# The copies of the transposed ternary weights move from VectorE to ScalarE

## The chip, the cores and the metric

The kernel runs on the 8 cores of one Trainium2 chip, the same program on each, each with 2 of the 16 sequences. All cores prepare the same weights for themselves. The metric is the device time of the slowest core in microseconds (us).

## The reference

A layer: layernorm, then a Nystrom attention and a feed-forward block with quantized weights and activations, both added to x.

```python
x  = L0_attn_x                                   # (16, 2048, 1024)
xn = _layernorm(x)
x  = x + attn(xn, Wk, Wq, Wv, Wo, bo) + ffn(xn, w1, conv_w, conv_b, w2)

def weight_quant(w):                             # w1 is (4096, 1024), w2 is (1024, 4096)
    scale = 1.0 / clip(mean(abs(w)), 1e-05)
    return clip(round(w * scale), -1, 1) / scale

def ffn(x, w1, conv_w, conv_b, w2):
    h = einsum('bsd,hd->bsh', act_quant(x), weight_quant(w1))
    h = silu(depthwise_conv1d(h, conv_w, conv_b))
    return einsum('bsh,dh->bsd', act_quant(h), weight_quant(w2))
...
```

The change touches `weight_quant` alone: the ternary weights (-1, 0, 1) are made once, before both sequences, and are needed with their input dimension on the partitions, so they are transposed.

## The kernel before

A core first prepares weights, then runs five stages for each of its two sequences, with a barrier of all engines and all DMAs after the preparation and after each stage. The generator `prep_weights` casts the four attention matrices (32 pieces) while `phase_A` (layernorm and quantization of sequence 0) is emitted in between; by the time it comes to w1 and w2, phase A is over. Then `_tern_weight` runs for w1 and for w2, alone on the core.

`_tern_weight` works on chunks of 128 rows: 32 chunks of 128x1024 for w1, 8 chunks of 128x4096 for w2. It has two passes over the weights, each of which loads every chunk from HBM by a DMA on SP's queue into one of two buffers `wtmps[c % 2]`; the load of chunk c+1 is emitted before the work on chunk c, and waits until the buffer's last reader is done.

Pass 1: VectorE sums the absolute values of each chunk (L398). Then two small matmuls and some one-element operations (L404 to L440) give the scale. Pass 2, for each chunk c, emitted in this order:

1. ScalarE: `w * scale + C_RND` in place, so that the value is rounded (L453).
2. VectorE: subtract `C_RND`, write int16 `ti` (L457).
3. VectorE: clip to -1..1, write bf16 `tb` (L460).
4. TensorE: for each group of 8 blocks of 128x128, 8 transposes into one PSUM bank (L470). w1 has one group for a chunk, always in `pb[2]`; w2 has four, in `pb[2]` and `pb[3]` in turn.
5. VectorE: copy the group's 128x1024 bf16 from PSUM to SBUF, for w1 into the resident `w1t` (L479, a strided destination), for w2 into the buffer `stage` (L485).
6. w2 only: one DMA of `stage` to `w2t_sp` in HBM, issued from ScalarE's queue (L490, listed as L162 in the trace, the line of the DMA helper).

There is no planner: what an engine runs, and in which order, is the order in which these calls are emitted. The helper `op` puts, ahead of an instruction, a wait for each writer and reader of its buffers, those on the same engine included: the four copies of a w2 chunk all write `stage`, so each waits for the end of the one before. After w2 comes the barrier, and then `phase_B1` of sequence 0, whose first instruction is a memset (L697).

Of the kernel before, what the change touches and what calls it, by code (L numbers as in the profile page):

```python
# [46 lines left out]
class Builder:  # L47
# [331 lines left out]
    def _tern_weight(self, wd, nrows, ncol, is_w1, tern_bufs):  # L379
        nc = self.nc  # L380
        nch = nrows // 128
        wtmps, ti, tb, stage = (tern_bufs[k] for k in
                                ("wtmp", "ti", "tb", "stage"))
        absacc = Buf(self.sml.ap[:, 448:448 + nch], "absacc")
        if is_w1:
            self._absacc = absacc
        else:
            absacc = self._absacc
        def ldw(c):
            self.dma(Buf(wtmps[c % 2].ap[:, 0:ncol], "wtv"),  # L390
                     wd[c * 128:(c + 1) * 128, :], writes=(wtmps[c % 2],))

        ldw(0)
        for c in range(nch):
            if c + 1 < nch:
                ldw(c + 1)
            wtmp = wtmps[c % 2]
            self.op("dve", lambda c=c, wtmp=wtmp: nc.vector.reduce_sum(  # L398
                absacc.ap[:, c:c + 1], wtmp.ap[:, 0:ncol], axis=AX.X,
                apply_absolute_value=True),  # L400
                reads=[wtmp], writes=[absacc])
            yield
        ps = self.pb[0]
        self.op("pe", lambda: nc.tensor.matmul(  # L404
            ps.ap[:1, 0:nch], self.ones_col.ap, absacc.ap[:, 0:nch],
            start=True, stop=True),
            reads=[self.ones_col, absacc], writes=[ps])
        tot = Buf(self.sml.ap[:1, 1700:1701], "tot")
        self.op("dve", lambda: nc.vector.reduce_sum(
            tot.ap, ps.ap[:1, 0:nch], axis=AX.X), reads=[ps], writes=[tot])  # L410
        mean = Buf(self.sml.ap[:1, 1701:1702], "mean")
        self.op("dve", lambda: nc.vector.tensor_scalar(
            mean.ap, tot.ap, 1.0 / (nrows * ncol), 1e-5, ALU.mult, ALU.max),
            reads=[tot], writes=[mean])
        scale = Buf(self.sml.ap[:1, 1702:1703], "scale")
        self.op("dve", lambda: nc.vector.reciprocal(scale.ap, mean.ap),
                reads=[mean], writes=[scale])
        row2 = Buf(self.sml.ap[:1, 1704:1706], "row2")
        self.op("dve", lambda: nc.vector.tensor_copy(row2.ap[:, 0:1], scale.ap),
                reads=[scale], writes=[row2])  # L420
        self.op("dve", lambda: nc.vector.tensor_copy(row2.ap[:, 1:2], mean.ap),
                reads=[mean, row2], writes=[row2])
        ones_row = Buf(self.sml.ap[:1, 1708:1836], "ones_row")
        self.op("dve", lambda: nc.vector.memset(ones_row.ap, 1.0),
                writes=[ones_row])
        ps2 = self.pb[1]
        self.op("pe", lambda: nc.tensor.matmul(
            ps2.ap[:, 0:2], ones_row.ap, row2.ap, start=True, stop=True),
            reads=[ones_row, row2], writes=[ps2])
        if is_w1:  # L430
            self.w1_mw = Buf(self.sml2.ap[:, 229:230], "w1_mw")
            self.w1_sc = Buf(self.sml2.ap[:, 230:231], "w1_sc")
            mw_col, sc_col = self.w1_mw, self.w1_sc
        else:
            self.w2_mw = Buf(self.sml2.ap[:, 231:232], "w2_mw")
            self.w2_sc = Buf(self.sml2.ap[:, 232:233], "w2_sc")
            mw_col, sc_col = self.w2_mw, self.w2_sc
        self.op("dve", lambda: nc.vector.tensor_copy(sc_col.ap, ps2.ap[:, 0:1]),
                reads=[ps2], writes=[sc_col])
        self.op("dve", lambda: nc.vector.tensor_copy(mw_col.ap, ps2.ap[:, 1:2]),  # L440
                reads=[ps2], writes=[mw_col])
        if is_w1:
            self.cw2 = Buf(self.sml2.ap[:, 128:128 + 3 * NHC], "cw2")
            self.op("dve", lambda: nc.vector.tensor_scalar(
                self.cw2.ap, self.cw.ap, mw_col.ap, None, ALU.mult),
                reads=[self.cw, mw_col], writes=[self.cw2])
        nblk = ncol // 128
        ldw(0)
        for c in range(nch):
            if c + 1 < nch:  # L450
                ldw(c + 1)
            wtmp = wtmps[c % 2]
            self.op("act", lambda wtmp=wtmp: nc.scalar.activation(  # L453
                wtmp.ap[:, 0:ncol], wtmp.ap[:, 0:ncol], AF.Identity,
                scale=sc_col.ap, bias=self.crnd_col.ap),
                reads=[wtmp, sc_col, self.crnd_col], writes=[wtmp])
            self.op("dve", lambda wtmp=wtmp: nc.vector.tensor_scalar(  # L457
                ti.ap[:, 0:ncol], wtmp.ap[:, 0:ncol], C_RND, None,
                ALU.subtract), reads=[wtmp], writes=[ti])
            self.op("dve", lambda: nc.vector.tensor_scalar(  # L460
                tb.ap[:, 0:ncol], ti.ap[:, 0:ncol], -1.0, 1.0, ALU.max,
                ALU.min), reads=[ti], writes=[tb])
            for g0 in range(0, nblk, 8):
                gn = min(8, nblk - g0)
                psb = self.pb[2 + (g0 // 8) % 2]
                pbf = psb.ap.bitcast(BF16)
                emits = []
                for j in range(gn):
                    blk = g0 + j
                    emits.append(lambda j=j, blk=blk: nc.tensor.transpose(  # L470
                        pbf[:, j * 128:(j + 1) * 128],
                        tb.ap[:, blk * 128:(blk + 1) * 128],
                        self.idb_sb.ap))
                self.op("pe", emits, reads=[tb, self.idb_sb], writes=[psb])
                if is_w1:
                    dst = self.w1t.ap.rearrange("p (kc d) -> p kc d", kc=KC)[
                        :, g0:g0 + gn, c * 128:(c + 1) * 128]
                    self.op("dve", lambda dst=dst, gn=gn, pbf=pbf:
                            nc.vector.tensor_copy(  # L479
                                dst, pbf[:, 0:gn * 128].rearrange(  # L480
                                    "p (kc d) -> p kc d", kc=gn)),
                            reads=[psb], writes=[self.w1t])
                else:
                    self.op("dve", lambda g0=g0, gn=gn, pbf=pbf:
                            nc.vector.tensor_copy(  # L485
                                stage.ap[:, g0 * 128:(g0 + gn) * 128],
                                pbf[:, 0:gn * 128]),
                            reads=[psb], writes=[stage])
            if not is_w1:
                self.dma(self.w2t_sp[:, :, c * 128:(c + 1) * 128].rearrange(  # L490
                    "hc p c2 -> p hc c2"),
                    stage.ap[:, 0:NHC * 128].rearrange(
                        "p (hc c2) -> p hc c2", hc=NHC),
                    reads=(stage,), q="act")
            yield
# [1123 lines left out]
```

How the kernel before makes its waits and increments, by code:

```python
    def _wait(self, e, tok):  # L98
        if tok is None:
            return
        key = id(tok.sem)
        w = self.waited[e]
        if w.get(key, -1) >= tok.val:
            return
        self._engine(e).wait_ge(tok.sem, tok.val)
        w[key] = tok.val
# [5 lines left out]
    def op(self, e, emits, reads=(), writes=()):  # L112
        if not isinstance(emits, (list, tuple)):
            emits = [emits]
        reads = [self._buf(b) for b in reads]
        writes = [self._buf(b) for b in writes]
        for b in reads:
            for t in b.ready:
                self._wait(e, t)
        for b in writes:
            for t in b.users:
                self._wait(e, t)
            for t in b.ready:
                self._wait(e, t)
        instr = None
        for em in emits:
            instr = em()
        sem = self.esem[e]
        self.ecnt[e] += 1
        instr.then_inc(sem, 1)
        tok = Tok(sem, self.ecnt[e])
        for b in reads:
            b.users.append(tok)
        for b in writes:
            b.ready = [tok]
            b.users = []
        return tok
# [1 line left out]
    def dma(self, out, in_, reads=(), writes=(), q="sp", wait=(), **kw):  # L139
# [19 lines left out]
        i = self.dnext  # L159
        self.dnext = (self.dnext + 1) % len(self.dsem)
        self._wait(e, Tok(self.dsem[i], self.dcnt[i]))
        instr = self._engine(e).dma_start(out=oap, in_=iap, **kw)
        self.dcnt[i] += 16
        instr.then_inc(self.dsem[i], 16)
        tok = Tok(self.dsem[i], self.dcnt[i])
        for b in reads:
```

## Time and profile before

| | |
|---|---|
| median of 3 runs | 4310.58 us (4310.55 to 4321.11) |
| the profiled execution: time | 4308.99 us |
| its span on the slowest core (core 0) | 4307.2 us |
| spans of the 8 cores | 4282.4 to 4307.2 us |
| VectorE busy | 2044.2 us, 47% of the span |
| ScalarE busy | 1237.2 us, 29% of the span |
| TensorE busy | 2158.3 us, 50% of the span |

The profile's times count from the first instruction of the span. The stages of interest lie at 396 to 501 us (pass 2 of w1), 501 to 564 us (pass 1 of w2) and 564 to 676 us (pass 2 of w2). "Before [x]" in a row is the idle time of the engine just ahead of the instruction, and what ended it. Engines are PE (TensorE), PEld (its weight loads), DVE (VectorE), ACT (ScalarE), SP; ACTq and SPq are the queues from which DMAs are issued.

### The profile page before, as it was taken

What the parts mean: (1) busy time and instruction counts of PE and PEld (TensorE: products, weight loads), DVE (VectorE), ACT (ScalarE), POOL (GpSimd) and SP (SyncE); (2) the same over time, 40 slices, a digit from 0 to 9 for tenths busy, and PEclk for the clock granted to TensorE, in tenths of its full rate; (3) what the DMA queues carried; (4) which work ended last, traced back from release to release, by engine and by line L of the source; (5) the groups of instructions that cost most, each with busy time, mean ns of one, the idle gap of its engine ahead of it and who ended that gap; (6) DMA issues with size and microseconds to landing.
All of it is one profiled execution on the core that took longest, in us unless ns stands there. A gap on an engine that the chain in (4) does not pass through costs nothing.

```text
span 4307.2 us, 46860 instructions; the slowest of 8 cores (4282.4 to 4307.2 us)
## 1 busy us (share of the span) xinstructions
PE 2158.3 (50%) x12052; PEld 1178.5 (27%) x12052; DVE 2044.2 (47%) x3629; ACT 1237.2 (29%) x1933; POOL 12.8 (0%) x132
## 2 busy tenths in 40 slices
PE   0101225876523556565655117767424556565654
PEld 0000113546512222222212114447312212222212
DVE  2224544333243284949484434343242375857573
ACT  4531221120022061525251451210021152424241
POOL 0000000000000000000000000000000000000000
PEclk9999997985555798888988558975556789898988
DMA  5435682100101303030303221100102203131313
GB/s 138 132 122 187 213 250 59 38 28 0 42 1 30 108 1 106 35 106 35 106 35 96 83 69 45 40 16 1 42 1 64 74 18 98 42 99 44 97 37 108
DMA packets 212931, 305.82 MB, mean 71 GB/s; under 512 B 109596, under 2 KB 126142, under 8 KB 210376
## 3 DMA queue, kind: packets, MB, share of 16 engines
q1 hardware_dynamic: 73544, 197.94, 14.4%
q10 hardware_dynamic: 139136, 104.88, 8.8%
q8 instruction: 114, 1.87, 0.2%
q14 instruction: 137, 1.12, 0.1%
HBM read 244.02 MB, written 58.76 MB: 70 GB/s over the span
## 4 chain that ended last, share of the span: by engine, by line
PE 29%; DVE 27%; DMA 19%; issue 15%; ACT 8%; DVEq 1%; ACTq 1%; SPq 0%; POOL 0%; POOLq 0%
DMA mix<-w2t_sp 8%; PE pb L1522 7%; PE pb L1012 5%; PE pb L775 5%; DVE scr L1413 4%; DVE scr L1365 4%; PE pb L804 3%; DMA h<-w 3%; PE pb L1231 2%; DMA h<-wo_sp 2%; DVE scr L1440 1%; DMA h<-q_sp 1%; PE pb L470 1%; DVEq L105 1%; DVE mix L1554 1%
## 5 line engine op out<-in xcount | busy, mean ns | idle before, releaser
L1357 PE MATMUL pb<-mix,w1t 128*128 128x512 bf16 x2048 | 529.9, 410 | 300.5 <-DVE scr L1365 284.2
L1522 PE MATMUL pb<-mix,h 128*128 128x512 bf16 x2048 | 509.1, 396 | 243.0 <-DMA mix<-w2t_sp 172.8
L1357 PEld LDWEIGHTS pb<-mix,w1t 128*128 128x128 bf16 x2048 | 197.2, 103 | 633.1 <-issue 471.4
L1400 ACT ACTIVATE scr<-scr,sml 128x512 f32<-128x512 f32 x256 | 208.1, 813 | 515.0 <-DVE scr L1394 302.5
L1522 PEld LDWEIGHTS pb<-mix,h 128*128 128x128 bf16 x2048 | 204.3, 100 | 545.8 <-issue 390.4
L1509 ACT CAST h<-scr 128x512 bf16<-128x512 int16 x256 | 147.1, 615 | 553.0 <-PE pb L1522 430.1
L775 PE MATMUL pb<-mix,h 128*128 128x512 bf16 x1024 | 257.6, 416 | 80.8 <-DVE h L785 58.3
L1506 DVE TENSOR_SCALAR scr<-scr 128x512 int16<-128x512 f32 x256 | 109.3, 427 | 313.6 <-ACT h L1509 290.3
L1012 PE MATMUL pb<-h 128*128 128x64 f32 x960 | 213.7, 422 | 49.1 <-DVE h L1037 22.2
L1012 PEld LDWEIGHTS pb<-h 128*128 128x128 f32 x960 | 207.7, 332 | 60.1 <-issue 60.1
L1424 ACT ACTIVATE h<-scr 128x512 f32<-128x512 f32 x256 | 161.2, 630 | 187.7 <-DVE scr L1419 187.7
L1419 DVE SCALAR_TENSOR_TENSOR scr<-scr,sml 128x512 f32<-128x512 f32 x256 | 192.3, 751 | 27.8 <-DVE scr L1413 1.4
L630 PE MATMUL pb<-idf_sb,sml 128*1 128x128 f32 x32 | 11.9, 372 | 377.7 <-ACT scr L623 196.1
L1502 DVE TENSOR_TENSOR scr<-h,scr 128x512 f32<-128x512 f32 x256 | 175.3, 685 | 39.7 <-DMA scr<-s2r_sp 39.7
L1413 DVE SCALAR_TENSOR_TENSOR scr<-scr,sml 128x512 f32<-128x512 f32 x256 | 192.3, 751 | 2.0 <-issue 1.5
L1365 DVE TENSOR_TENSOR scr<-pb,invbc 128x512 f32<-128x512 f32 x256 | 175.4, 685 | 12.7 <-PE pb L1357 11.0
L1231 PE MATMUL pb<-h,mix 128*128 128x512 bf16 x512 | 141.6, 419 | 63.3 <-DMA h<-wo_sp 38.7
L775 PEld LDWEIGHTS pb<-mix,h 128*128 128x128 bf16 x1024 | 106.2, 106 | 226.5 <-issue 131.7
L453 ACT ACTIVATE h<-h,cons,sml 128x1024 f32<-128x1024 f32 (+1 forms) x40 | 70.1, 1752 | 278.8 <-DVE sml L440 151.0
L1151 ACT ACTIVATE scr<-pb,sml 128x512 bf16<-128x512 f32 x32 | 22.0, 687 | 426.1 <-DVE sml L1141 423.0
L812 ACT CAST h<-pb 128x512 bf16<-128x512 f32 x64 | 37.4, 585 | 353.6 <-PE pb L804 352.1
L470 PE MATMUL pb<-idb_sb,h 128*128 128x128 bf16 x512 | 61.6, 305 | 147.7 <-DVE h L460 145.3
(204 smaller groups left out, 2840.6 us busy)
## 6 DMA issues: line engine op xcount, KB each, us to landing
h<-w SPq DMA_DIRECT2D x64, 512.0 KB
h<-w SPq DMA_DIRECT2D x16, 2048.0 KB
mix<-w2t_sp SPq DMA_DIRECT2D x128, 256.0 KB
mix<-w2t_sp ACTq DMA_DIRECT2D x128, 256.0 KB
h<-wo_sp ACTq DMA_DIRECT2D x64, 256.0 KB
h<-x SPq DMA_DIRECT2D x32, 512.0 KB
out<-mix SPq DMA_DIRECT2D x32, 512.0 KB
scr<-x SPq DMA_DIRECT2D x16, 512.0 KB
```

The source lines that it names most:

```text
L775: w512=w512: nc.tensor.matmul(psq.ap[:, 0:w512], wb.ap[:, kc * 128:(kc + 1) * 128], xn_fm.ap[:, kc * L + n4 * 512: kc * L + n4 * 512 + w51 ...
L1012: emits.append(lambda pr=pr: nc.tensor.matmul(psd.ap[:, pr * M:(pr + 1) * M], lhsbd.ap[:, pr * 128:(pr + 1) * 128], rhs.ap[:, pr * M:(pr + ...
L1231: ps_w=ps_w, wo_b=wo_b: nc.tensor.matmul(ps_w.ap, amix.ap.rearrange("p (pr t) -> p pr t", pr=NPAIR)[:, kc, tb * 128:tb * 128 + 128], wo_b. ...
L1357: nc.tensor.matmul(psm.ap[:, 0:TT], self.w1t.ap[:, kc * DH + hc * 128: kc * DH + hc * 128 + 128], xq_b.ap[:, kc * TT:(kc + 1) * TT], start ...
L1365: nc.vector.tensor_tensor(hcur.ap[:, 1:TT + 1], psm.ap[:, 0:TT], self.invbc_b.ap[:, t0:t0 + TT], ALU.mult),
L1400: nc.scalar.activation(acc1.ap[:, 0:TT], hcur.ap[:, 1:TT + 1], AF.Identity, bias=self.cb.ap[:, hc:hc + 1], scale=self.cw2.ap[:, 3 * hc + 1 ...
L1413: nc.vector.scalar_tensor_tensor(acc2.ap[:, 0:TT], hcur.ap[:, 0:TT], self.cw2.ap[:, 3 * hc:3 * hc + 1], acc1.ap[:, 0:TT], ALU.mult, ALU.add),
L1419: nc.vector.scalar_tensor_tensor(acc3.ap[:, 0:TT], hcur.ap[:, 2:TT + 2], self.cw2.ap[:, 3 * hc + 2:3 * hc + 3], acc2.ap[:, 0:TT], ALU.mult ...
L1424: self.op("act", lambda hc=hc, acc3=acc3: nc.scalar.activation(h2.ap[:, hc * 512:hc * 512 + TT], acc3.ap[:, 0:TT], AF.Silu), reads=[acc3], ...
L1502: self.op("dve", lambda hc=hc, qa=qa: nc.vector.tensor_tensor(qa.ap[:, 0:TT], h2.ap[:, hc * 512:hc * 512 + TT], s2bc.ap[:, 0:TT], ALU.mult ...
L1509: self.op("act", lambda hc=hc, par=par: nc.scalar.copy(h2q[:, hc * 1024:hc * 1024 + TT], tqI[par].ap[:, 0:TT]), reads=[tqI[par]], writes=[ ...
L1522: ps_o=ps_o, wb=wb: nc.tensor.matmul(ps_o.ap, h2q[:, hc * 1024 + tb * 128: hc * 1024 + tb * 128 + 128], wb.ap[:, half * 512:half * 512 + 512],
```

## The change

The two copies out of PSUM in pass 2 (L479 for w1, L485 for w2), 32 instructions each, are issued on ScalarE (`nc.scalar.copy`) where they were on VectorE (`nc.vector.tensor_copy`). Operands, buffers, order of emission and everything else stay.

```diff
                 if is_w1:
                     dst = self.w1t.ap.rearrange("p (kc d) -> p kc d", kc=KC)[
                         :, g0:g0 + gn, c * 128:(c + 1) * 128]
-                    self.op("dve", lambda dst=dst, gn=gn, pbf=pbf:
-                            nc.vector.tensor_copy(
+                    self.op("act", lambda dst=dst, gn=gn, pbf=pbf:
+                            nc.scalar.copy(
                                 dst, pbf[:, 0:gn * 128].rearrange(
                                     "p (kc d) -> p kc d", kc=gn)),
                             reads=[psb], writes=[self.w1t])
                 else:
-                    self.op("dve", lambda g0=g0, gn=gn, pbf=pbf:
-                            nc.vector.tensor_copy(
+                    self.op("act", lambda g0=g0, gn=gn, pbf=pbf:
+                            nc.scalar.copy(
                                 stage.ap[:, g0 * 128:(g0 + gn) * 128],
                                 pbf[:, 0:gn * 128]),
                             reads=[psb], writes=[stage])
```

## Rows read from the trace of the kernel before

**Rows 1.** Windows: busy us and count of each engine, clock, DMA share, GB/s

```profile
395.00:501.00 106.00, 32.88 (x258) 25.21 (x258) 55.79 (x100) 39.68 (x32) 0.00 (x0) 1.00 0.51 165
501.00:564.00 63.00, 0.75 (x4) 0.61 (x4) 36.45 (x16) 0.37 (x1) 0.00 (x0) 1.00 0.79 283
```

**Rows 2.** Groups of instructions, shapes apart, 300 to 860 us

```profile
L453 ACT ACTIVATE h<-h,cons,sml 128x1024 f32<-128x1024 f32 x32 | 39.7, 1240 | 146.4 <-DVE sml L440 84.8 <-DMA h<-w 61.7
...
L479 DVE COPY w1t<-pb 128x1024 bf16<-128x1024 bf16 x32 | 22.1, 692 | 43.9 <-PE pb L470 43.9
```

**Rows 3.** Timeline, pass 2 of w1: its first and last scaling, one chunk between

```profile
396.09 1.24 ACT L453 ACTIVATE h<-h,cons,sml 128x1024 f32<-128x1024 f32 x1 [84.78 <-DVE sml L440]
...
441.09 1.24 ACT L453 ACTIVATE h<-h,cons,sml 128x1024 f32<-128x1024 f32 x1 [3.17 <-DMA h<-w]
...
442.50 0.69 DVE L457 TENSOR_SCALAR h<-h 128x1024 int16<-128x1024 f32 x1 [0.33 <-ACT h L453]
...
443.30 0.43 DVE L460 TENSOR_SCALAR h<-h 128x1024 bf16<-128x1024 int16 x1
...
443.98 1.01 PE L470 MATMUL pb<-idb_sb,h 128*128 128x128 bf16 x8 [2.60 <-DVE h L460]
445.10 0.69 DVE L479 COPY w1t<-pb 128x1024 bf16<-128x1024 bf16 x1 [1.37 <-PE pb L470]
445.70 0.69 DVE L457 TENSOR_SCALAR h<-h 128x1024 int16<-128x1024 f32 x1
...
493.77 0.68 DVE L457 TENSOR_SCALAR h<-h 128x1024 int16<-128x1024 f32 x1
...
496.20 1.24 ACT L453 ACTIVATE h<-h,cons,sml 128x1024 f32<-128x1024 f32 x1 [3.15 <-DMA h<-w]
```

**Rows 4.** Timeline, ScalarE alone, phase A of sequence 0

```profile
118.94 1.04 ACT L593 CAST sml<-sml 128x1024 bf16<-128x1024 int16 x1 [2.38 <-DVE sml L590]
120.07 1.04 ACT L595 CAST sml<-invbc 128x1024 bf16<-128x1024 f32 x1
121.02 1.00 ACT L618 COPY mix<-pb 128x1024 bf16<-128x1024 bf16 x1
121.92 1.01 ACT L623 COPY scr<-pb 128x1024 bf16<-128x1024 bf16 x1
...
123.71 0.25 ACT L634 COPY sml<-pb 1x128 f32<-1x128 f32 x1 [0.77 <-PE pb L630]
123.87 1.14 ACT L348 ACTIVATE h<-h,cons 128x1024 bf16<-128x1024 f32 x1
```

**Rows 5.** Timeline, a transpose and the ScalarE copy that waits for it

```profile
310.55 0.37 PE L630 MATMUL pb<-idf_sb,sml 128*1 128x128 f32 x1 [1.42 <-ACT sml L623]
311.06 0.25 ACT L634 COPY sml<-pb 1x128 f32<-1x128 f32 x1 [0.77 <-PE pb L630]
```

**Rows 6.** Timeline, the first sum of pass 1 of w2

```profile
504.82 4.42 DVE L398 TENSOR_REDUCE sml<-h 128x1 f32<-128x4096 f32 x1 [3.92 <-DMA h<-w]
```

**Rows 7.** Timeline, pass 2 of w2: one chunk, to the next scaling

```profile
598.98 0.69 DVE L485 COPY h<-pb 128x1024 bf16<-128x1024 bf16 x1 [1.44 <-PE pb L470]
...
599.93 1.87 PE L470 MATMUL pb<-idb_sb,h 128*128 128x128 bf16 x16 [0.27 <-DVE h L485]
601.11 0.69 DVE L485 COPY h<-pb 128x1024 bf16<-128x1024 bf16 x1 [0.58 <-PE pb L470]
601.97 0.69 DVE L485 COPY h<-pb 128x1024 bf16<-128x1024 bf16 x1 [0.16 <-DVE h L485]
602.74 0.37 ACTq L162 DMA_DIRECT2D w2t_sp<-h  x1
603.21 3.80 ACT L453 ACTIVATE h<-h,cons,sml 128x4096 f32<-128x4096 f32 x1 [9.39 <-DVE h L485]
```

**Rows 8.** The chain of work that ended last, longest pieces, 0 to 800 us: start, us, what

```profile
491.44 4.68 DMA h<-w
```

**Rows 9.** Groups of instructions, ScalarE alone, 0 to 700 us

```profile
L344 ACT ACT_TABLE_LOAD x1 | 1.3, 1283 | 8.2 <-DMA h<-Wk 8.2
```

## The prediction

> **What bounds the kernel now.** I read the windows first, to see which engines share the two stages that change. In pass 2 of w1 VectorE is busy 55.8 of 106 us and ScalarE 39.7 [rows 1]: no engine is full. So the question is which chain sets the pace. The groups by line give the costs of one instruction, and that ScalarE sat idle 61.7 us ahead of its scalings L453, each time until a load landed [rows 2]. That looks like room. The timeline says where it lies [rows 3]: L457 starts at 442.50 and, for the next chunk, at 445.70, 3.20 us apart, and in between VectorE, TensorE and VectorE take turns: L457, L460, eight transposes (443.98), copy (445.10), and nothing of it overlaps. ScalarE's scaling of the next chunk lies beside this chain. The whole of pass 2 of w1 has 31 periods between 396.09 and 496.20: 3.23 us each, 0.03 more than the chain because a load is sometimes late (441.09 and 496.20 are such cases: L457 had to wait for the scaling).
>
> In w2 the scaling isn't ahead of the copies: L453 at 603.21 starts after the last copy's end (602.66) and the store that ScalarE's queue issues behind it (602.74) [rows 7]. Each w2 chunk is one serial chain already.
>
> **The change, part by part.**
>
> *Engine order in w1.* On ScalarE's queue the copy of chunk c stands ahead of the scaling of chunk c+1. The copy waits for the transposes of c, they for L460, that for L457, that for the scaling of c. What is queued behind the waiting copy is the next scaling, and VectorE waits for that. So the five steps, of which the scaling was hidden, become one ring. Its period, start to start:
> - scaling to L457: 442.50 - 441.09 = 1.41 us, a case in which VectorE really waited for ScalarE [rows 3]
> - L457 to L460: 443.30 - 442.50 = 0.80
> - L460 to the transposes: 443.98 - 443.30 = 0.68
> - transposes to the copy: 445.10 - 443.98 = 1.12 to VectorE, 0.11 of it after TensorE's end. To ScalarE the same hand-over is 311.06 - (310.55 + 0.37) = 0.14 [rows 5], so 1.15
> - copy to the next scaling: ScalarE already makes copies of this shape and type out of PSUM, 1.00 to 1.01 us long, in L618 (strided destination like `w1t`) and L623. The next one starts 0.90 us after [rows 4], since nothing makes it wait for the end. That the follower may be an activation from SBUF too is shown by L348, which starts 0.16 after a 0.25 copy out of PSUM, again 0.09 before its end. I take 0.90.
>
> Sum 4.94 us, 1.71 above 3.23. Over 30 periods the end of L457 of chunk 30 goes from 494.45 (493.77 + 0.68) to 396.09 + 30 x 4.94 + 1.41 + 0.68 = 546.4: +51.9 us. That instruction is the right one to carry on from, because it frees the buffer into which pass 1 of w2 loads first. Bounds: if the hand-over to L457 took 0.09 like that of L595 behind L593 (120.07 against 118.94 + 1.04 = 119.98 [rows 4]) and the one to the copy 1.12 as now, 4.83, so +48.6; if the scaling had to wait for the copy's end and 0.09 more (as L595 does behind L593), 5.13, so +57.6.
>
> *Late loads.* The 0.03 us of a period that they cost is already given back in this sum: a load now has most of two periods (7.8 us after the buffer is freed) and needs under 5 (4.68 in the slowest shown [rows 8]).
>
> *Pass 1 of w2.* The first sum starts at 504.82 [rows 6], 10.4 us after the freeing L457, and the stage runs at 283 GB/s with the DMAs 79% busy [rows 1]: it is paced by loads, and moves as a block. One gain: of those 10.4 us about 1.8 overlapped with the load of the last w1 chunk (491.44 to 496.12 [rows 8]), which the longer period will have landed before. At 283 GB/s its remaining 0.19 MB are 0.7 us. VectorE's sum no longer stands behind the last copy, but it waits for the load anyway. Stage start and end: +51.2.
>
> *Copies in w2.* I replay the chunk of [rows 7] with copies of 1.01 us, copy 0 0.03 later than now for the hand-over, a wait of 0.09 for the one before (all write `stage`), and 0.26 from a copy's end to the next transposes in its bank (599.67 to 599.93). Copy 0: 599.01 to 600.02. Copy 1: 600.11 to 601.12. Group 2 transposes from 600.28, copy 2 1.21 later (601.11 - 599.93 = 1.18 now, and 0.03): 601.49 to 602.50. Group 3 from 601.38 (bank free), copy 3: 602.59 to 603.60, against 602.66 before: +0.94 a chunk, 7.5 us for eight. Bounds: 0.32 for one exposed copy is 2.6 us; four copies each 0.32 longer, none hidden, is 10.2.
>
> *Issue of the store and the barrier* stay: 0.08 from the copy's end to the issue [rows 7], and the same last store ahead of the barrier. Copy 0 of a chunk also needs `stage` free, that is the former chunk's store landed. At 598.98 it is TensorE that it waited for [rows 7], so the store had landed, hidden by the scaling, L457 and L460. Without that cover each us that a store is late would cost 7 us; with longer chunks the cover grows.
>
> *VectorE* loses 64 copies of 0.692 us, 44.3 us busy [rows 2]. Nothing else waits for VectorE in these stages, so it is worth nothing. ScalarE gains 64 x 1.01 = 64.6 us.
>
> A copy out of PSUM on ScalarE takes 1.01 us against 0.692 on VectorE [rows 2, 4]. The Trainium skill (Advanced Engine Details and Errata, The Read-Write Bubble) says that ScalarE lies nearer to PSUM and VectorE nearer to SBUF, and to use them accordingly, which speaks for the move. Its effect can only be on the fixed part: by it alone the sum would be some us smaller; the rows have the copy 0.32 us longer in all, so the trace does not bear the rule out for this shape. Another rule speaks against it: a ScalarE queue is a strict FIFO (the Trainium skill, PSUM — Partial Sum Buffer, Engine vs sequencer instructions), and the w2 scaling that stands behind the store's issue agrees.
>
> Sum: 51.2 + 7.5 = 58.7 us on the profiled execution's 4308.99 = 4367.7 us. The median of the runs shown is 1.6 above that execution. I predict 4368.
>
> **Rivals.**
>
> *Faster: ScalarE scales ahead.* If the scaling of c+1 got past the waiting copy, VectorE's ring would lose the copy, and w1 would go at the pace of its loads: at 283 GB/s a chunk of 0.524 MB takes 1.85 us, ScalarE's own work 1.24 + 1.01 - 0.09 = 2.16. At best 3.23 - 2.16 = 1.07 us x 31 = -33, and +7.5 in w2: 4283 us. For it: the busy shares. Against: emission order, and the pacing of rows 7. It decides only if the scaling's start comes ahead of the copy's. 2 in 100.
>
> *Same: the copy fills ScalarE's idle.* 61.7 us idle over 31 chunks is 2.0 us each, twice the copy. If the copy sat in there at the old period of 3.23, only w2's part would be left: +7.5, 4316 us, within 0.3%. Against: that idle lies before the transposes whose result the copy needs. 2 in 100.
>
> *Slower still: a table load at each switch.* ScalarE would alternate between Identity (L453) and Copy. A table load is 1.283 us [rows 9]; two for each w1 chunk are 82 us more, and w2 adds 21: about 4470. Against: casts and Identity activations alternate in phase A [rows 4] and none is loaded there between them. 2 in 100.
>
> **How the numbers follow.** 94 in 100 for the ring. A measurement of this kernel tells about 0.3% (13 us) from no change, and the forecast is 57 above the median. Low end: 48.6 - 0.7 + 2.6 = 50.5 gives 4359.5; high end: 57.6 - 0.7 + 10.2 = 67 gives 4376; with 1.6 between execution and median and the runs' own spread of some us, 4356 to 4380. Slower 0.96, same 0.02, faster 0.02.
>
> **What the profile after would show.** ScalarE's groups at the two copy lines, x32 each at 1.00 to 1.02 us; L453 of w1 starting 0.90 after each copy, at a period of 4.94, and no longer waiting for loads; VectorE idle ahead of L457 until L453; the last w1 scaling near 549, the first w2 scaling near 615, the first memset of B1 near 735 (676 before). Wrong would be: a period under 4.8 or over 5.15, w2 chunks not about 0.9 us longer, a table load among them, or stages after B1 of another length, for example by another granted clock.

## The result, and the profile after

The changed kernel is slower: 4380.06 us median (4371.17 to 4416.57, 10 runs) against 4314.4 (4308.84 to 4365.13, 10 runs of the kernel before, the three shown ahead among them). The ratio is 1.0153 with a 95% interval of 1.0129 to 1.0178, about +66 us. I had forecast 4368 and a range up to 4380: the direction and the mechanism held, the size was too small by 12 us and the median lies just outside the range. The profiled execution took 4371.17 us.

The page's first part, the changed kernel on its slowest core, core 7:

```profile
span 4369.4 us, 47003 instructions; the slowest of 8 cores (4346.7 to 4369.4 us)
PE 2162.8 (49%) x12052; PEld 1182.6 (27%) x12052; DVE 2002.8 (46%) x3565; ACT 1302.9 (30%) x1997; POOL 12.8 (0%) x132
```

64 instructions moved: VectorE has 41 us less work and ScalarE 66 us more, and the kernel is longer by as much as it is for another reason, which the busy times don't show. The groups of instructions by line, shapes apart, from 300 to 860 us, answer to [rows 2]:

```profile
L453 ACT ACTIVATE h<-h,cons,sml 128x1024 f32<-128x1024 f32 x32 | 39.8, 1244 | 86.9 <-DVE sml L440 86.9
L479 ACT COPY w1t<-pb 128x1024 bf16<-128x1024 bf16 x32 | 32.4, 1013 | 95.8 <-PE pb L470 95.8
L485 ACT COPY h<-pb 128x1024 bf16<-128x1024 bf16 x32 | 32.4, 1013 | 48.2 <-PE pb L470 46.8
...
L457 DVE TENSOR_SCALAR h<-h 128x1024 int16<-128x1024 f32 x32 | 22.2, 694 | 120.4 <-ACT h L453 120.4
...
L460 DVE TENSOR_SCALAR h<-h 128x1024 bf16<-128x1024 int16 x32 | 13.7, 427 | 5.5 <-DVE h L457 5.4
L460 DVE TENSOR_SCALAR h<-h 128x4096 bf16<-128x4096 int16 x8 | 9.8, 1227 | 2.8 <-DVE h L457 2.7
```

ScalarE's 61.7 us of waiting for loads [rows 2] are gone from L453's row. In their place it waits 95.8 us for the transposes ahead of its copies, and VectorE waits 120.4 us for the scaling, 3.8 us for each chunk. A copy takes 1.013 us. The last two rows were not forecast: L460 waits for L457, the instruction just ahead of it on its own engine.

The timeline of pass 2 of w1 on core 7, one chunk and the start of the next, answers to [rows 3]:

```profile
400.13 1.24 ACT L453 ACTIVATE h<-h,cons,sml 128x1024 f32<-128x1024 f32 x1
401.55 0.69 DVE L457 TENSOR_SCALAR h<-h 128x1024 int16<-128x1024 f32 x1 [3.85 <-ACT h L453]
402.42 0.43 DVE L460 TENSOR_SCALAR h<-h 128x1024 bf16<-128x1024 int16 x1 [0.17 <-DVE h L457]
...
403.20 1.01 PE L470 MATMUL pb<-idb_sb,h 128*128 128x128 bf16 x8 [4.13 <-DVE h L460]
404.36 1.01 ACT L479 COPY w1t<-pb 128x1024 bf16<-128x1024 bf16 x1 [2.99 <-PE pb L470]
405.27 1.24 ACT L453 ACTIVATE h<-h,cons,sml 128x1024 f32<-128x1024 f32 x1
```

This is the forecast ring: nothing overlaps, and the next scaling starts 0.91 us after the copy. But the period is 5.14 us where I had 4.94. The steps, start to start, are 1.42, 0.87, 0.78, 1.16 and 0.91, against 1.41, 0.80, 0.68, 1.15 and 0.90 in the forecast: L457 to L460 and L460 to the transposes are the ones that grew.

Pass 2 of w2 on core 7, one chunk, answers to [rows 7]:

```profile
625.64 3.80 ACT L453 ACTIVATE h<-h,cons,sml 128x4096 f32<-128x4096 f32 x1 [0.55 <-ACT h L485]
629.61 2.29 DVE L457 TENSOR_SCALAR h<-h 128x4096 int16<-128x4096 f32 x1 [10.52 <-ACT h L453]
632.29 1.23 DVE L460 TENSOR_SCALAR h<-h 128x4096 bf16<-128x4096 int16 x1 [0.38 <-DVE h L457]
...
633.87 1.86 PE L470 MATMUL pb<-idb_sb,h 128*128 128x128 bf16 x16 [9.95 <-DVE h L460]
635.03 2.11 ACT L485 COPY h<-pb 128x1024 bf16<-128x1024 bf16 x2 [5.59 <-PE pb L470]
...
637.45 2.11 ACT L485 COPY h<-pb 128x1024 bf16<-128x1024 bf16 x2 [0.31 <-PE pb L470]
639.64 0.37 ACTq L162 DMA_DIRECT2D w2t_sp<-h  x1
640.11 3.80 ACT L453 ACTIVATE h<-h,cons,sml 128x4096 f32<-128x4096 f32 x1 [0.55 <-ACT h L485]
```

The first half of the chunk before, whose second half is in [rows 7] (core 0):

```profile
590.01 3.80 ACT L453 ACTIVATE h<-h,cons,sml 128x4096 f32<-128x4096 f32 x1 [9.39 <-DVE h L485]
593.92 2.29 DVE L457 TENSOR_SCALAR h<-h 128x4096 int16<-128x4096 f32 x1 [4.45 <-ACT h L453]
596.32 1.23 DVE L460 TENSOR_SCALAR h<-h 128x4096 bf16<-128x4096 int16 x1
...
597.80 1.86 PE L470 MATMUL pb<-idb_sb,h 128*128 128x128 bf16 x16 [9.20 <-DVE h L460]
```

A chunk takes 640.11 - 625.64 = 14.47 us; before, the same distance is 603.21 - 590.01 = 13.20. From L457 to L460 it is 2.68 us against 2.40, where the instruction itself takes 2.29 as before.

Whole runs of any one kernel here differ by some tens of us between executions, and the stages after the preparation differ between cores by as much. So I compare stages. Each number of this table is the median over the 8 cores of a distance in the timeline of one profiled execution: 31 periods of w1 (first to last L457), from there to the first L457 of w2, 7 chunks of w2, and from the last L457 to the first memset of `phase_B1`. The last columns are the sum's distance from the kernel before, and the ratio of whole runs with its interval.

| kernel | w1 | to w2 | w2 | to B1 | sum, against before | ratio of runs |
|---|---|---|---|---|---|---|
| before | 99.9 | 66.3 | 92.8 | 15.8 | | |
| the change | 159.4 | 63.8 | 101.2 | 17.6 | +67.2 | 1.0153 (1.0129 to 1.0178) |
| w1_only | 159.4 | 65.8 | 92.6 | 16.4 | +59.4 | 1.0103 (1.0044 to 1.0163) |
| w2_only | 99.6 | 66.3 | 101.4 | 17.8 | +10.3 | 1.0005 (0.9972 to 1.0038) |
| before_order_ring | 150.7 | 63.4 | 92.8 | 15.8 | +47.9 | 1.0132 (1.0079 to 1.0185) |
| before_4waits | 108.0 | 66.6 | 94.8 | 16.1 | +10.7 | 1.0039 (1.0007 to 1.0071) |
| fold_waits | 146.7 | 64.0 | 97.2 | 17.1 | +50.2 | 1.0110 (1.0033 to 1.0188) |
| scale_first | 92.8 | 66.7 | 86.9 | 25.2 | -3.2 | 0.9974 (0.9940 to 1.0008) |
| before_scale_first | 99.6 | 65.5 | 87.2 | 17.3 | -5.2 | 1.0017 (0.9984 to 1.0051) |
| before_sf_2stage | 99.8 | 66.8 | 75.5 | 15.8 | -16.9 | 0.9960 (0.9920 to 1.0000) |
| sf_2stage | 94.3 | 66.8 | 74.9 | 18.0 | -20.7 | 0.9944 (0.9916 to 0.9973) |
| sf_2stage_4loads | 79.7 | 72.8 | 75.4 | 18.0 | -28.9, and 24.5 less ahead of w1 than sf_2stage | 0.9873 (0.9840 to 0.9905) |

The w2 column holds a control: where no edit touches w2 (w1_only, before_order_ring) it is 92.6 and 92.8, as before. In the kernels with the scaling first, L457 runs ahead of the copies, so part of a chunk's work moves from the w2 column behind the last L457; for them the two last columns have to be added.

The change loses 67.2 us in the stages that it touches, and the runs say 66, with an interval of 56 to 77. In the two profiled executions the median span of the 8 cores grows by 63.2 us: those 67, with 1.4 less ahead of the first L457 of w1 and 2.6 less from B1 on. So the loss lies in these stages, and what follows them did not get longer.

### The profile page after: what moved, and what is told of

Read it like the earlier page. It is cut to its first block, busy times and chain, and to the rows that moved or that the text cites. A ratio compares the mean times of both kernels' runs of the same rounds, so it can differ in the third digit from the quotient of the medians.

```text
span 4369.4 us, 47003 instructions; the slowest of 8 cores (4346.7 to 4369.4 us)
## 1 busy us (share of the span) xinstructions
PE 2162.8 (49%) x12052; PEld 1182.6 (27%) x12052; DVE 2002.8 (46%) x3565; ACT 1302.9 (30%) x1997; POOL 12.8 (0%) x132
## 4 chain that ended last, share of the span: by engine, by line
PE 28%; DVE 27%; DMA 18%; issue 16%; ACT 9%; DVEq 1%; ACTq 1%; SPq 0%; POOL 0%; POOLq 0%
DMA mix<-w2t_sp 8%; PE pb L1522 7%; PE pb L1012 5%; DVE scr L1413 4%; PE pb L775 4%; DVE scr L1365 4%; PE pb L804 3%; DMA h<-w 2%; PE pb L1231 2%; DMA h<-wo_sp 2%; ACT h L453 2%; DMA h<-q_sp 1%; DVE scr L1440 1%; PE pb L470 1%; DVEq L105 1%
## 5 line engine op out<-in xcount | busy, mean ns | idle before, releaser
L457 DVE TENSOR_SCALAR h<-h 128x1024 int16<-128x1024 f32 (+1 forms) x40 | 40.6, 1014 | 198.6 <-ACT h L453 198.6
```

## The experiments

**The two parts alone.** Each of these two kernels makes one of the two edits; no other line changes.

```diff
 w1_only
-                    self.op("dve", lambda dst=dst, gn=gn, pbf=pbf:
-                            nc.vector.tensor_copy(
+                    self.op("act", lambda dst=dst, gn=gn, pbf=pbf:
+                            nc.scalar.copy(
 w2_only
-                    self.op("dve", lambda g0=g0, gn=gn, pbf=pbf:
-                            nc.vector.tensor_copy(
+                    self.op("act", lambda g0=g0, gn=gn, pbf=pbf:
+                            nc.scalar.copy(
```

> Only the 32 copies of w1 on ScalarE, those of w2 stay on VectorE. The ring theory puts most of the change here: a w1 period of 5.14 us against 3.23 before, 1.91 x 31 = 59 us, less about 1 us that pass 1 of w2 wins back, so the kernel is 58 us slower than before, and a w2 chunk stays at 13.2 us. The theory that the copy sits in ScalarE's idle expects a period of 3.23 and no difference. The theory of a table load at each switch expects a period above 7.

> Only the 32 copies of w2 on ScalarE. The ring theory expects a w1 period of 3.23 us as before and a w2 chunk of 14.47 us against 13.20, 10 us in all; as each chunk is serial before and after, nothing else moves. If w1 and w2 each cost what they cost in the full change, the two kernels' differences add up to its 66 us.

w1_only: 4360.41 us median, a w1 period of 159.4 / 31 = 5.14 us, w2 as before. w2_only: 4313.87 us, w1 as before, w2 +10.6 us, of which 2.0 behind the last L457. As 0.25% of the kernel that is less than whole runs tell; the stage shows it, the ratio does not. The parts add up to 69.7 us by stages against 67.2 together.

**Order alone.** The copy stays on VectorE, and the scaling waits for it:

```diff
 ...
             wtmp = wtmps[c % 2]
+            if is_w1:
+                for t in self.w1t.ready:
+                    self._wait("act", t)
             self.op("act", lambda wtmp=wtmp: nc.scalar.activation(
```

> The kernel before, copies on VectorE, with one wait added on ScalarE: the scaling of a w1 chunk waits until VectorE has copied the chunk before. That is the order which ScalarE's queue imposes in the changed kernel, with the shorter copy and without the move. If the order is the cause, the w1 period is 1.41 + 0.80 + 0.68 + 1.12 + 0.79 (the 0.69 us copy and 0.1 for the hand-over) = 4.80 us, 49 us in w1; the remaining 0.34 of the changed kernel's 5.14 are then its longer copy and its added waits. If ScalarE's slower copy or some cost of ScalarE out of PSUM were the cause, the period stays near 3.2.

Its timeline in w1, core 0 (the added lines shift the numbers: L456 is the scaling, L460 and L463 are L457 and L460, L482 the copy):

```profile
434.93 1.24 ACT L456 ACTIVATE h<-h,cons,sml 128x1024 f32<-128x1024 f32 x1 [3.61 <-DVE w1t L482]
436.34 0.69 DVE L460 TENSOR_SCALAR h<-h 128x1024 int16<-128x1024 f32 x1 [1.56 <-ACT h L456]
437.14 0.43 DVE L463 TENSOR_SCALAR h<-h 128x1024 bf16<-128x1024 int16 x1
...
437.82 1.01 PE L473 MATMUL pb<-idb_sb,h 128*128 128x128 bf16 x8 [3.84 <-DVE h L463]
438.94 0.69 DVE L482 COPY w1t<-pb 128x1024 bf16<-128x1024 bf16 x1 [1.37 <-PE pb L473]
439.78 1.24 ACT L456 ACTIVATE h<-h,cons,sml 128x1024 f32<-128x1024 f32 x1 [3.61 <-DVE w1t L482]
```

4355.10 us, a period of 4.85, where 4.80 was expected. With the copy on its old engine and at its old length, 50.8 of the 59.5 us that w1 loses are there. So the order is most of the loss. The other 0.29 us of a period lie in three steps that are longer in the changed kernel, copy to scaling (0.07), L457 to L460 (0.07) and L460 to the transposes (0.10), and 0.05 in the two hand-overs left. And from L456 on every step has the length that I had forecast: 1.41, 0.80, 0.68, 1.12. So a long idle of TensorE, 3.84 us here and 4.13 in the changed kernel, is not what made its step grow there. VectorE's idle is shorter here (1.56 against 3.85 us), so for its step this run doesn't decide; the next two do.

**Waits.** The helper leaves a wait out if the same engine has already waited for that value. Before, VectorE's copy waited for TensorE, so the next L460 needed no wait for TensorE (which reads `tb`). With the copy gone L460 makes that wait itself, one in w1 and four in w2 (the four groups are four reads of `tb`, each with its own value). Likewise TensorE now waits for ScalarE's semaphore for its bank, where VectorE's value covered it; L457 in w2 for VectorE's own; and the copy in w1 for ScalarE's own. They are satisfied long before, but they stand behind the wait for the input. One kernel adds such waits to the kernel before, the other reorders and merges them in the changed one:

```diff
 before_4waits
+            for t in ti.ready:
+                self._wait("dve", t)
+            for v in (1, 2, 3, 4):
+                nc.vector.wait_ge(self.esem["pe"], v)
             self.op("dve", lambda: nc.vector.tensor_scalar(
                 tb.ap[:, 0:ncol], ti.ap[:, 0:ncol], -1.0, 1.0, ALU.max,
                 ALU.min), reads=[ti], writes=[tb])
 ...
 fold_waits, in op(), for pass 2 alone (in place of the waits that stood there)
+            need = {}
+            for b in writes:
+                for t in b.users + b.ready:
+                    if t is not None and (id(t.sem) not in need or
+                                          need[id(t.sem)].val < t.val):
+                        need.pop(id(t.sem), None)
+                        need[id(t.sem)] = t
+            for b in reads:
+                for t in b.ready:
+                    o = need.pop(id(t.sem), t)
+                    need[id(t.sem)] = t if t.val >= o.val else o
+            for t in need.values():
+                self._wait(e, t)
```

> The kernel before, with four more waits between L457 and L460 in each chunk of pass 2, all for values that TensorE's semaphore has long passed. If a passed wait costs 0.07 to 0.08 us where it stands between an input's arrival and its reader, the distance from L457 to L460 grows from 0.80 to 1.10 us in w1 and from 2.40 to 2.70 in w2, the w1 period from 3.2 to 3.5 and the kernel by 12 us (31 and 8 times 0.3). If passed waits are free and the longer hand-overs of the changed kernel come from idle engines, nothing moves.

> The full change, but in pass 2 each instruction waits once for each semaphore (for the highest value alone), and first for buffers that are free long since, last for its inputs. No dependence is dropped. The theory that the part of the period that I had missed is waits of about 0.07 us each that stand between an input's arrival and its reader expects: L457 to L460 from 0.87 back to 0.80 us in w1 and from 2.68 to 2.40 in w2, L460 to the transposes from 0.78 to 0.68, scaling to L457 from 1.42 to 1.35, so a w1 period of 4.87 and a w2 chunk of 14.0, 12 us off the full change. The rival theory, that engines are slower to answer after a longer idle, expects 5.14 and 14.47 as in the full change.

The timeline of before_4waits, w1, core 0 (L464 is L460 with the waits ahead of it):

```profile
433.74 0.68 DVE L457 TENSOR_SCALAR h<-h 128x1024 int16<-128x1024 f32 x1
...
434.81 0.43 DVE L464 TENSOR_SCALAR h<-h 128x1024 bf16<-128x1024 int16 x1 [0.38 <-DVE h L457]
```

L457 to L464 is 1.07 us against 0.80 [rows 3]: 0.27 for four waits, 0.068 each. The 0.38 us of idle is also what L460 has in w2 of the changed kernel (632.29 above), where four waits came in. The stages grow by 8.1 us in 31 chunks of w1 and 2.0 in 7 of w2; the runs give 1.0039. All the stages together grow by 10.7 us where 12 were expected. That is the price of a passed wait on VectorE.

The timeline of fold_waits, w1, core 0 (L472 is the scaling, L476 and L479 are L457 and L460, L498 the copy):

```profile
472.38 1.24 ACT L472 ACTIVATE h<-h,cons,sml 128x1024 f32<-128x1024 f32 x1
473.72 0.69 DVE L476 TENSOR_SCALAR h<-h 128x1024 int16<-128x1024 f32 x1 [3.51 <-ACT h L472]
474.52 0.43 DVE L479 TENSOR_SCALAR h<-h 128x1024 bf16<-128x1024 int16 x1
...
475.10 1.01 PE L489 MATMUL pb<-idb_sb,h 128*128 128x128 bf16 x8 [3.72 <-DVE h L479]
476.20 1.01 ACT L498 COPY w1t<-pb 128x1024 bf16<-128x1024 bf16 x1 [2.58 <-PE pb L489]
477.11 1.24 ACT L472 ACTIVATE h<-h,cons,sml 128x1024 f32<-128x1024 f32 x1
```

A period of 4.73 us, lower than the expected 4.87: the steps are 1.34, 0.80, 0.58, 1.10, 0.91. The edit also moved waits that the kernel before already had behind an input, TensorE's for its own semaphore among them, which I hadn't counted: 0.41 us for five waits in a period: one each ahead of L457, L460 and the copy (0.06 to 0.08 us), and two ahead of the transposes (0.20 together). VectorE sits idle 3.51 us ahead of L457 here, nearly as long as in the changed kernel, and L457 to L460 is back at 0.80: so its idle is not the cause either. In w2 a chunk takes 97.2 / 7 = 13.89 us (expected 14.0). By whole runs, 4361.31 us, their interval (1.0033 to 1.0188) takes in the change's; its stages are 17 us shorter.

**The order turned round.** The scaling of c+1 is emitted behind L460 of c, ahead of the copies of c, in the changed kernel (scale_first) and in the kernel before (before_scale_first, where only w2 is affected). `scale_w(c)` is the instruction of L453 for chunk c, and the line with `ALU.min` is the end of L460:

```diff
             wtmp = wtmps[c % 2]
-            self.op("act", lambda wtmp=wtmp: nc.scalar.activation(
-                wtmp.ap[:, 0:ncol], wtmp.ap[:, 0:ncol], AF.Identity,
...
+            if c == 0:
+                scale_w(0)
...
                 ALU.min), reads=[ti], writes=[tb])
+            if c + 1 < nch:
+                scale_w(c + 1)
             for g0 in range(0, nblk, 8):
```

> The full change with the scaling of chunk c+1 emitted ahead of the copies of chunk c. The ring theory says that the order on ScalarE's queue is the whole loss of w1 and that this takes it away: a w1 period of about 3.0 us (a load takes 3.8 us from its issue, the scaling 1.4 and L457 0.7, for two chunks in turn), and a w2 chunk of 9 to 11 us, as the scaling now runs beside VectorE and the store. About 60 us off w1 and 28 to 44 off w2 against the full change, so 4275 to 4290 us, faster than before by 0.5 to 1%. If the copy's own length or its place on ScalarE were the loss, w1 would keep most of the 59 us.

> The kernel before, copies on VectorE, with only the scaling of chunk c+1 emitted ahead of the copies and of the store of chunk c. The w1 stage has this order already: its period stays at 3.2 us. In w2 the scaling no longer stands behind the store's issue; after the run with the copies on ScalarE the next limit is the single buffer that the store reads: 7 us from its issue to its landing and 3.7 us of copies, so 11 to 12.5 us a chunk against 13.2, 6 to 15 us off the kernel, 4290 to 4300. If the queue order were not the limit of w2, 13.2.

scale_first: 4300.25 us, where 4275 to 4290 were expected; that is some 1.8% below the change, and by the runs no different from the kernel before. The 59.5 us of w1 are gone and 7 more (92.8 against 99.9, 2.99 us a chunk as expected), with the copies still on ScalarE. before_scale_first stays at 99.6 in w1, so these 7 us are what taking the copy off VectorE is worth once the order is right. In w2 I expected 9 to 11 us for a chunk and it takes 12.4; and as 25.2 us lie behind the last L457 against 15.8, w2 and the tail together take 112.1 us, less than in the change (118.8) but more than before (108.6). The waits of scale_first on core 0 from 550 to 640 us (engine, tile and line waited, for whom: us, times, longest) say what is late next (L493 is the copy, L478 the transposes):

```profile
PE pb L478 <- ACT h L493: 44.0, 8, 10.6
...
ACT h L493 <- DMA w2t_sp<-h: 27.8, 7, 7.1
```

The copy waits for the store of the chunk before, which reads the one buffer `stage`. That cover, which I had noted as hidden, is gone once chunks overlap. Core 0 is the best case: on the other cores the same waits are 35 to 39 us. before_scale_first has the same limit (36 to 45 us of waits for the store): 12.5 us for a chunk, w2 and tail 104.5, 4309.59 us. I had expected 4290 to 4300; the stages are 5 us shorter than before, and the runs show no difference.

**Two buffers for the store.** Both kernels with a second `stage`, used in turn. It lies where the casts of the attention matrices were, and the copies of the first two chunks wait for those:

```diff
-            stage=Buf(h2.ap[:, 12288:14336].bitcast(BF16), "tstage"),
+            stage=[Buf(h2.ap[:, 12288:14336].bitcast(BF16), "tstage0"),
+                   Buf(h2.ap[:, 14336:16384].bitcast(BF16), "tstage1")],
...
+            stage = stages[c % 2]
```

> The same with two buffers for the store, in turn. VectorE then carries L457, L460, the wait for the first transposes and four copies in a row, 2.4 + 1.5 + 1.2 + 3.7 = 8.8 us; the loads need 7.4 us for 2 MB and the store comes on top. I expect 9 to 11 us for a w2 chunk, so 20 to 30 us off the kernel before. If it stays at 11 to 12.5, the store's buffer was not the limit but the DMAs themselves.

> The full change with the scaling first and two buffers for the store. In w2 ScalarE carries a scaling, four copies and the store's issue, 3.8 + 4.5 + 0.55 = 8.9 us, loads and store as in the run with copies on VectorE, so 9 to 11 us for a chunk against 12.4 with one buffer; w1 stays at 3.0. 15 to 25 us off the run with the scaling first and one buffer, about 1% faster than before. If ScalarE were the worse place for the copies even out of the ring, this run would be slower than the one with two buffers and copies on VectorE by more than the 7 us that w1 gives it.

A w2 chunk takes 10.8 us with the copies on VectorE and 10.7 with them on ScalarE; with the tail w2 takes 91.3 and 92.9 us. So out of the ring the engine makes next to no difference here. The runs: 4292.36 us (0.9960, the interval touches 1) and 4284.59 us (0.9944). The first is 12 us below the kernel before by the medians and 17 by the stages, where 20 to 30 were expected.

What holds w2 now is the store again, in another way. On core 0 of sf_2stage the first chunks are 8.8 us apart, and then one store takes long to issue:

```profile
574.87 0.37 ACTq L162 DMA_DIRECT2D w2t_sp<-h  x1
...
583.63 9.69 ACTq L162 DMA_DIRECT2D w2t_sp<-h  x1
...
593.43 3.80 ACT L453 ACTIVATE h<-h,cons,sml 128x4096 f32<-128x4096 f32 x1 [9.87 <-issue]
```

The scaling stands behind that issue on ScalarE's queue. Issues of 1.4 to 10.3 us occur on all 8 cores of both kernels, and none over 0.5 us in scale_first, the change or the kernel before. In w2 the DMAs are busier too, 88 to 94% of the time on the cores of sf_2stage against 74 to 84% in scale_first. What makes an issue wait, and whether another queue for the store would help, no run shows.

What is left in w1 stands in the chain of work that ended last, sf_2stage, core 0 (start, us, what):

```profile
399.61 3.66 DMA h<-w
...
403.35 1.25 ACT h L453
...
404.76 0.70 DVE h L466
...
405.58 3.76 DMA h<-w
```

A load, the scaling, L457 (L466 here), and then the next load into the same buffer: 5.97 us for two chunks.

**Four load buffers for w1** on top of that (buffers of 128x1024, three loads ahead):

```diff
 ...
+        if is_w1:
+            wtmps = [Buf(self.h2.ap[:, i * 2048:i * 2048 + 1024], "tws%d" % i)
+                     for i in range(4)]
+        nw = len(wtmps)
...
-            if c + 1 < nch:
-                ldw(c + 1)
+            if c + nw - 1 < nch:
+                ldw(c + nw - 1)
```

> The best version so far (copies on ScalarE, scaling first, two store buffers) with four buffers for the loads of w1 in place of two, in both passes. If w1's two passes go at the pace of a load's 3.7 us from issue to landing and its buffer's reuse, pass 1 goes from 2.6 to about 1.9 us a chunk (0.52 MB at 283 GB/s) and pass 2 from 3.04 to 2.45, the ring through the one PSUM bank (2.46 us from transposes to transposes where no load was late). 15 to 20 us off each, together 4245 to 4255 us. If the rate of the DMAs is the limit already, neither moves.

4249.25 us, ratio 0.9873 (0.9840 to 0.9905): faster than both kernels. The first L457 comes at 365.0 us in the median of the cores against 389.5 in sf_2stage (15 to 20 us were expected of pass 1), and 31 periods of w1 take 79.7 us, 2.57 each (2.45 expected). Some 6 us of it are given back between the two weights (72.8 against 66.8); why is open.

## Why the prediction was right and where it was wrong

*The ring in w1* was right in kind: turning the order round takes all of it away, imposing it on the old engine brings 50.8 of 59.5 us back. *The step that failed* is its size: "L457 to L460: 443.30 - 442.50 = 0.80" and "L460 to the transposes: 443.98 - 443.30 = 0.68", sum 4.94. I took these two from a stretch in which the copy on VectorE had made other instructions' waits unnecessary, and looked for hand-overs only where an engine changed. They measured 0.87 and 0.78. The hand-over to the copy and the one to L457 grew by 0.01 each, and with 0.01 more from the copy to the scaling the period is 5.14. Over 31 periods w1 is 59.5 us longer, where 53 were forecast. That a passed wait on VectorE costs 0.068 us is shown by before_4waits, and that these hand-overs shrink with the waits by fold_waits; I had left the waits that the helper would emit out of the step altogether. The bound of 5.13 was from another cause (a wait for the copy's end), and that cause did not occur: the scaling starts 0.91 after the copy.

*Copies in w2*: forecast +0.94 us for a chunk, measured +1.27. The four copies themselves were nearly right: 639.56 - 635.03 = 4.53 us from the first start to the last end, 4.59 forecast, 3.68 before. The rest is a term that the forecast did not have, waits again: +0.28 between L457 and L460, +0.06 ahead of L457, +0.10 from L460 to the transposes; in fold_waits all three are gone (2.40, 3.91 and 1.37 us, against 2.40, 3.91 and 1.48 before). With the tail it is 10.2 us (101.2 + 17.6 against 92.8 + 15.8) where 7.5 were forecast.

*Pass 1 of w2 moves as a block*: right. From L457 of the last w1 chunk to the first of w2 it is 2.5 us shorter, 1.8 in my numbers (53.0 of shift at the one, 51.2 at the other). On core 0, from which I had read, the same distance was 3.7 us above the other cores' median before, so its own shift would have misled. I gave the overlap of its first load with the last w1 load as 1.8 us; by the trace it is 1.5 (issue at 494.63, landing at 496.12), which moves the sum by 0.1 us.

*VectorE's freed time is worth nothing, and no table is loaded at a switch*: right for this change; with the order turned round the freed time is worth 7 us in w1. The copies take 1.013 us, and ScalarE's one table load up to 860 us is L344's, as before [rows 9].

*The sum*: 58.7 forecast, 67.2 by stages, 65.7 between the medians of the runs, so 7 us of the 12 are the size of the loss. The other 5.4 us are the starting point: I added to an execution of 4308.99 us, and the ten runs of the kernel before have a median of 4314.4. My range allowed only 1.6 us for that, plus "some us". That the median came out only 0.06 us above the range is chance; by the stages the sum was 8.5 us short.

*The rivals*: "ScalarE scales ahead" was no description of this change, but it was a good one of the kernel with the order turned round, which came out at 92.8 us in w1, short of the 2.16 us a chunk that I gave it, because loads into two buffers allow 2.99. "The copy fills ScalarE's idle" fails on w1_only, the table load on the period.

## What to carry to other kernels

Idle time of an engine is room only where the instruction to be moved can run: here ScalarE's 61.7 us lay before the data existed, and a move to an in-order queue puts everything behind it into a ring. Emit the next chunk's first step ahead of this chunk's last one, then look for the buffer that is late next (here the store's in w2, and the loads' in w1), and add up the stage and its tail, since work that runs ahead at one line can end no earlier at the last. When an instruction changes engine, list the waits again on both engines: a wait that it made for others must now be made by someone, and a wait for inputs should stand last, behind those for buffers long free.

## What the runs showed of the hardware that was not expected

A wait on a semaphore that has long passed costs VectorE 0.068 us if it stands between the input's arrival and its reader (four cost 0.27 us in before_4waits), in a chain of instructions of 0.4 to 1.2 us. On TensorE two such waits were worth 0.20 us and on ScalarE one 0.06 (fold_waits). A ScalarE copy that leaves PSUM as bf16, 128x1024, is 0.32 us longer than VectorE's, and this showed only where the copy stands in a serial chain: with the order turned round and two store buffers, a w2 chunk takes 10.7 and 10.8 us on the two engines. With two store buffers the issue of a store on ScalarE's queue took up to 10.3 us where it otherwise takes 0.37, and the instruction behind it waited.
